# Second MLP layer and overlap-add as one convolution on TensorE, and patch rows that are loaded earlier, in the last phase of a two-layer image kernel

## The reference, cut to what matters

```python
def _mlp(x, W1, b1, W2, b2):
    h = jax.nn.relu(x @ W1.T + b1)
    return h @ W2.T + b2
B, C, H, W = x.shape                       # 16, 32, 64, 64
...
t = pat.reshape(B, C * 9, H * W).transpose(0, 2, 1)
t = t + _dmha(_ln2(t), Wr, Wqkv, Wp, bp)   # attention: the phase before
t = t + _mlp(_ln2(t), W1, b1, W2, b2)      # 288 -> 72 -> 288
y = t.transpose(0, 2, 1).reshape(B, C, 9, H, W)
out = jnp.zeros((B, C, H + 2, W + 2), x.dtype)
idx = 0
for i in range(3):
    for j in range(3):
        out = out.at[:, :, i:i + H, j:j + W].add(y[:, :, idx])
        idx += 1
return out[:, :, 1:H + 1, 1:W + 1]
...
x = x + _L1_conv_ref(_gn(x), ...)
```

## Time and profile before

| | us |
|---|---|
| median of 3 runs | 12895.44 |
| lowest, highest of them | 12892.05, 12903.24 |
| profiled execution | 12904.24 |
| its span, first to last instruction | 12902.4 |
| fold phase: first product of `hide` to the last `out` | 12141.63 to 12896.39 |
| one sample in it | 46.97 |

### The profile page before, as it was taken

How to read it: one execution, slowest core, us unless ns; L and a number is a source line. 1 busy time by engine, 2 the same in 40 slices (tenths; PEclk the granted TensorE clock), 3 DMA queues, 4 the chain that set the end, 5 groups by cost and what they waited for, 6 DMA issues and landing times. The chain is left out here.

```text
span 12902.4 us, 255523 instructions
## 1 busy us (share of the span) xinstructions
PE 12303.8 (95%) x73276; PEld 4675.7 (36%) x73276; DVE 9188.1 (71%) x17067; ACT 7592.3 (59%) x15286; POOL 3414.9 (26%) x3268
## 2 busy tenths in 40 slices
PE   6999999999993799999999999999999999999899
PEld 2333333333331233333333333333333333333233
DVE  6777777777776677777777777777777777777311
ACT  4666666666663366666666666666666666666411
POOL 4777777767772000000000000000000000000143
PEclk9999999999996799999999999999999999999999
DMA  3111111101104332232232232232232233232255
GB/s 78 22 20 18 22 19 19 22 17 21 22 15 131 74 72 67 68 73 67 67 74 67 66 75 67 66 75 67 65 75 68 65 74 69 65 73 68 68 122 111
DMA packets 853483, 772.61 MB, mean 60 GB/s; under 512 B 587092, under 2 KB 621492, under 8 KB 840884
## 3 DMA queue, kind: packets, MB, share of 16 engines
q1 hardware_dynamic: 850612, 747.43, 25.5%
q10 hardware_dynamic: 1536, 8.39, 0.3%
HBM read 510.63 MB, written 244.96 MB: 59 GB/s over the span
## 5 line engine op out<-in xcount | busy, mean ns | idle before, releaser
L1547 DVE TENSOR_REDUCE a_big<-a_mp 128x1 f32<-128x512 f32 x8192 | 5219.2, 684 | 1826.1 <-PE a_mp L1381 1807.4
L1467 ACT ACTIVATE a_ex<-a_sc 128x512 f32<-128x512 f32 x8192 | 4426.3, 601 | 1935.5 <-PE a_sc L1369 1930.6
L1381 PE MATMUL a_mp<-a_ks,a_qs 108*128 108x512 bf16 x8192 | 3131.1, 383 | 39.7 <-DMA a_ks<-qk_parts 24.9
L1369 PE MATMUL a_sc<-a_qs,a_ks 111*128 111x512 bf16 x8192 | 3124.5, 383 | 6.8 <-ACT a_ex L1467 4.5
L893 DVE TENSOR_TENSOR r_prod<-r_pg,r_win 128x512 f32<-128x512 f32 x2816 | 1846.1, 683 | 783.2 <-PE r_pg L618 438.6
L546 POOL TENSOR_TENSOR r_prod<-r_temp,r_win 128x512 f32<-128x512 f32 x1792 | 2095.8, 1189 | 1158.9 <-ACT r_temp L845 954.5
L1283 POOL TENSOR_TENSOR a_pieces<-a_left,a_pieces 128x512 bf16<-128x512 f32 x256 | 295.5, 1154 | 7323.9 <-ACT a_pieces L1453 7323.9
L1395 PE MATMUL a_po<-a_ex,a_va 128*32 128x512 f32 x16384 | 2182.0, 605 | 1.6 <-ACT a_oc L1473 0.9
L1369 PEld LDWEIGHTS a_sc<-a_qs,a_ks 111*128 111x128 bf16 x8192 | 794.9, 97 | 2477.4 <-ACT a_ex L1467 1767.8
L1381 PEld LDWEIGHTS a_mp<-a_ks,a_qs 108*128 108x128 bf16 x8192 | 803.1, 98 | 914.1 <-DVE a_big L1547 238.3
L845 ACT COPY r_temp<-r_pg 128x512 f32<-128x512 f32 x1792 | 975.3, 590 | 77.2 <-PE r_pg L618 38.6
(11 more groups left out here) (185 smaller groups left out, 11641.8 us busy)
## 6 DMA issues: line engine op xcount, KB each, us to landing
a_qs<-qk_parts SPq DMA_DIRECT2D x768, 144.0 KB
a_ks<-qk_parts SPq DMA_DIRECT2D x768, 144.0 KB
qk_parts<-a_pieces SPq DMA_DIRECT2D x128, 768.0 KB, 5.2
f_t<-mixed SPq DMA_DIRECT2D x48, 1536.0 KB, 16.6
a_tw<-second SPq DMA_DIRECT2D x512, 128.0 KB, 3.0
mixed<-a_t SPq DMA_DIRECT2D x256, 256.0 KB, 2.1
r_win<-first SPq DMA_DIRECT2D x128, 280.5 KB, 4.9
a_zw<-layered SPq DMA_DIRECT2D x192, 144.0 KB, 12.0
```

Source lines behind the costliest of these rows:

```text
L1369: pe.matmul(sc[k % BANKS][:, :], ks[0:KROWS + NPART, p.h, head, 128 * kb:128 * kb + 128], qs[0:KROWS + NPART, p.h, head, CHUNK * qb:CHUNK ...
L1381: pe.matmul(mp[k % BANKS][:, :], qs[0:KROWS, p.h, head, 128 * q:128 * q + 128], ks[0:KROWS, p.h, head, CHUNK * half:CHUNK * half + CHUNK], ...
L1467: nc.scalar.activation(ex[:, k % RING, :], sc[k % BANKS][:, :], ACT.Exp, scale=scale).then_inc(exped.sem, 1)
L1547: nc.vector.tensor_reduce(big[:, x % 2, k // 2:k // 2 + 1], mp[k % BANKS][:, :], AX_X, ALU.max).then_inc(maxed.sem, 1)
```

## The change

The second layer and the folding become one convolution: `fold` now has, ahead of the twelve products with `sel`, 36 products that read `hidden` shifted by patch row i and patch column j with the 96 by 32 part of W2 for (i, j), into the same `pf[q]`. `unhide`, the PSUM tiles `pw` and VectorE's sum into `u` go away. `three` takes the place of `u`: it holds all eight chunks with an empty column left and right, and is what `sel` reads. `hidden` becomes 66 by 66 and is held twice, for two samples. `ph` has four banks, where it had two.

The semaphore of the load is divided: `t_in` counts the three transfers of `t`, `x_in` the four of the image. SyncE's loop waits for the last sum of `three` of sample p, issues the loads of `t` for p + 2, then stores p, then loads the image for p + 2. GpSimd's last sum waits for the last product of the first layer, so that both readers of `t` are done by then. VectorE zeroes the wider tiles at the start.

```diff
-        def unhide(p, k):
-            pe.wait_ge(h_done.sem, h_done.at(p.n, min(k + 2, CHUNKS)))
-            pe.wait_ge(u_done.sem, u_done.at(p.n, k - 1))
-            for i in range(3):
-                first = (CROWS * k + 2 - i) * IMG
-                last = pe.matmul(pw[k % 2][0:ROWS3, :], w2[:, i, :], hidden[:, first:first + CHUNK],
-                                 start=i == 0, stop=i == 2)
-            last.then_inc(w_made.sem, 1)
-
         def fold(p, q):
-            pe.wait_ge(u_done.sem, u_done.at(p.n, LANES * (q + 1)))
+            pe.wait_ge(h_done.sem, h_done.at(p.n, min(LANES * (q + 1) + 1, CHUNKS)))
+            pe.wait_ge(summed.sem, summed.at(p.n, LANES * (q + 1)))
             pe.wait_ge(out_done.sem, out_done.at(p.n, q - 1))
+            for j in range(3):
+                for i in range(3):
+                    for l in range(LANES):
+                        row = CROWS * (LANES * q + l) + 2 - i
+                        pe.matmul(pf[q][C * l:C * l + C, :].rearrange("p (a b) -> p a b", b=IMG), w2[:, i, C * j:C * j + C],
+                                  hidden[:, p.h, row:row + CROWS, 2 - j:2 - j + IMG], start=i == j == 0, stop=False,
+                                  tile_position=(0, C * l))
             for j in range(3):
                 for l in range(LANES):
                     last = pe.matmul(pf[q][C * l:C * l + C, :].rearrange("p (a b) -> p a b", b=IMG), sel[:, j, :],
-                                     u[:, LANES * q + l, :, 2 - j:2 - j + IMG], start=j == 0, stop=j == 2,
+                                     three[:, LANES * q + l, :, 2 - j:2 - j + IMG], start=False, stop=j == 2,
                                      tile_position=(0, C * l))
...
         def sample(p):
-            for k in range(CHUNKS + 2):
-                if k < CHUNKS:
-                    hide(p, k)
-                if k == 2 and not (isinstance(p.n, int) and p.n == 0):
+            for k in range(CHUNKS):
+                hide(p, k)
+                if k == 1 and not (isinstance(p.n, int) and p.n == 0):
                     fold(p.to(-1), 1)
-                if k == CHUNKS - 1:
+                if k == CHUNKS - 2:
                     fold(p, 0)
-                if k >= 2:
-                    unhide(p, k - 2)
...
             with sp.Fori(0, samples // 2 - 1) as i:
                 for h in range(2):
-                    store(Pass(2 * i + h, h, i))
+                    p = Pass(2 * i + h, h, i)
+                    sp.wait_ge(summed.sem, summed.at(p.n, CHUNKS))
                     load(Pass(2 * i + 2 + h, h, i + 1))
+                    store(p)
+                    load_image(Pass(2 * i + 2 + h, h, i + 1))
...
-                pool.wait_ge(u_done.sem, u_done.at(p.n, k - 3))
-                nc.gpsimd.tensor_tensor(three[:, k % 4, :], two[:, :], t[:, p.h, 2, rows[2]],
+                pool.wait_ge(folded.sem, folded.at(p.n, k // LANES - 1))
+                if k == CHUNKS - 1:
+
+                    pool.wait_ge(h_made.sem, h_made.at(p.n, CHUNKS))
+                nc.gpsimd.tensor_tensor(three[:, k, :, 1:IMG + 1], two[:, :].rearrange("p (a b) -> p a b", b=IMG),
+                                        t[:, p.h, 2, rows[2]].rearrange("p (a b) -> p a b", b=IMG),
                                         ALU.add).then_inc(summed.sem, 1)
...
-        link(nc.vector.memset(hidden[:, :], 0.0))
-        link(nc.vector.memset(hidden[64:ROWS3, IMG:IMG + PIX], 1.0))
-        link(nc.vector.memset(u[:, :, :, :], 0.0))
+        link(nc.vector.memset(hidden[:, :, :, :], 0.0))
+        for h in range(2):
+            link(nc.vector.memset(hidden[64:ROWS3, h, 1:IMG + 1, 1:IMG + 1], 1.0))
...
             for k, of in enumerate((rstd, bias)):
                 nc.vector.tensor_copy(coef[0:HID, p.h, k:k + 1], of[0:HID, bass.ds(p.n, 1)]).then_inc(coef_ready.sem, 1)
-            for k in range(CHUNKS):
-                dve.wait_ge(w_made.sem, w_made.at(p.n, k + 1))
-                dve.wait_ge(summed.sem, summed.at(p.n, k + 1))
-                if k % LANES == 0:
-
-                    dve.wait_ge(folded.sem, folded.at(p.n, k // LANES - 1))
-                nc.vector.tensor_tensor(u[:, k, :, 1:IMG + 1], pw[k % 2][0:ROWS3, :].rearrange("p (a b) -> p a b", b=IMG),
-                                        three[:, k % 4, :].rearrange("p (a b) -> p a b", b=IMG),
-                                        ALU.add).then_inc(u_done.sem, 1)
-                if k == 0 and not (isinstance(p.n, int) and p.n == 0):
-                    finish(p.to(-1), 1)
-                if k == CHUNKS - 2:
-                    finish(p, 0)
+            dve.wait_ge(x_in[p.h].sem, x_in[p.h].at(p.m, 64))
+            if not (isinstance(p.n, int) and p.n == 0):
+                finish(p.to(-1), 1)
+            finish(p, 0)
```

More of the change, by code:

```diff
@@ L1599, in fold_phase @@
     t = sb("t", [ROWS3, 2, 3, PAD * IMG])
-    hidden = sb("hidden", [ROWS3, PAD * IMG])
-    three = sb("three", [ROWS3, 4, CHUNK])
+    hidden = sb("hidden", [ROWS3, 2, PAD, PAD])
     two = sb("two", [ROWS3, CHUNK])
-    u = sb("u", [ROWS3, CHUNKS, CROWS, PAD])
+    three = sb("three", [ROWS3, CHUNKS, CROWS, PAD])
     x1 = sb("x1", [128, 2, 2, CHUNK])
@@ L1623, in fold_phase @@
     coef = sb("coef", [ROWS3, 2, 2])
-    ph = [ctx.enter_context(nc.psum_tensor(f"f_ph{i}", [128, CHUNK], F32)) for i in range(2)]
-    pw = [ctx.enter_context(nc.psum_tensor(f"f_pw{i}", [128, CHUNK], F32)) for i in range(2)]
+    ph = [ctx.enter_context(nc.psum_tensor(f"f_ph{i}", [128, CHUNK], F32)) for i in range(4)]
     pf = [ctx.enter_context(nc.psum_tensor(f"f_pf{i}", [128, CHUNK], F32)) for i in range(2)]
@@ L1637, in fold_phase @@
     coef_ready = Signal(sem("coef_ready"), 2)
-    loaded = [Signal(sem(f"loaded{h}"), 16 * 7) for h in range(2)]
+    t_in = [Signal(sem(f"t_in{h}"), 48) for h in range(2)]
+    x_in = [Signal(sem(f"x_in{h}"), 64) for h in range(2)]
     h_made = Signal(sem("h_made"), CHUNKS)
     h_done = Signal(sem("h_done"), CHUNKS, 1)
-    w_made = Signal(sem("w_made"), CHUNKS)
     paired = Signal(sem("paired"), CHUNKS, 1)
     summed = Signal(sem("summed"), CHUNKS, 1)
-    u_done = Signal(sem("u_done"), CHUNKS, 1)
     folded = Signal(sem("folded"), 2, 1)
@@ L1669, in load, with load_image @@
                 sp.dma_start(t[:, p.h, i, IMG:IMG + PIX].rearrange("p (u x) -> p u x", u=4),
-                             src).then_inc(loaded[p.h].sem, 16)
+                             src).then_inc(t_in[p.h].sem, 16)
+        def load_image(p):
             image = total[bass.ds(C * p.n, C), :].rearrange("c (q l x) -> c l q x", l=LANES, x=CHUNK)
             for l in range(LANES):
-                sp.dma_start(x1[C * l:C * l + C, p.h, :, :], image[:, l, :, :]).then_inc(loaded[p.h].sem, 16)
+                sp.dma_start(x1[C * l:C * l + C, p.h, :, :], image[:, l, :, :]).then_inc(x_in[p.h].sem, 16)
         def store(p):
@@ L1679, in store @@
                 sp.dma_start(image[:, l, :, :], out[C * l:C * l + C, p.h, :, :]).then_inc(stored[p.h].sem, 16)
-        sp.wait_ge(edged, 6)
-        load(Pass(0, 0, 0))
-        load(Pass(1, 1, 0))
+        sp.wait_ge(edged, 7)
+        for h in range(2):
+            load(Pass(h, h, 0))
+            load_image(Pass(h, h, 0))
         if samples > 2:
@@ L1706, in hide @@
             if k == 0:
-                pe.wait_ge(loaded[p.h].sem, loaded[p.h].at(p.m, 16 * 7))
-            pe.wait_ge(h_done.sem, h_done.at(p.n, k - 1))
+                pe.wait_ge(t_in[p.h].sem, t_in[p.h].at(p.m, 48))
+            pe.wait_ge(h_done.sem, h_done.at(p.n, k - 3))
             for i in range(3):
                 first = (CROWS * k + 1) * IMG
-                last = pe.matmul(ph[k % 2][0:HID, :], w1[:, i, :], t[:, p.h, i, first:first + CHUNK],
+                last = pe.matmul(ph[k % 4][0:HID, :], w1[:, i, :], t[:, p.h, i, first:first + CHUNK],
                                  start=i == 0, stop=i == 2)
             last.then_inc(h_made.sem, 1)
-        def unhide(p, k):
-            pe.wait_ge(h_done.sem, h_done.at(p.n, min(k + 2, CHUNKS)))
-            pe.wait_ge(u_done.sem, u_done.at(p.n, k - 1))
-            for i in range(3):
-                first = (CROWS * k + 2 - i) * IMG
-                last = pe.matmul(pw[k % 2][0:ROWS3, :], w2[:, i, :], hidden[:, first:first + CHUNK],
-                                 start=i == 0, stop=i == 2)
-            last.then_inc(w_made.sem, 1)
         def fold(p, q):
-            pe.wait_ge(u_done.sem, u_done.at(p.n, LANES * (q + 1)))
+            pe.wait_ge(h_done.sem, h_done.at(p.n, min(LANES * (q + 1) + 1, CHUNKS)))
+            pe.wait_ge(summed.sem, summed.at(p.n, LANES * (q + 1)))
             pe.wait_ge(out_done.sem, out_done.at(p.n, q - 1))
+            for j in range(3):
[5 more added lines that the diff above has]
+                                  tile_position=(0, C * l))
             for j in range(3):
@@ L1765, in sample @@
                 act.wait_ge(h_made.sem, h_made.at(p.n, k + 1))
-                first = (CROWS * k + 1) * IMG
```

(10 more changed lines are left out.)

3 lines of the change are left out of this document (1 added, 2 removed).

## The result

| | before | after |
|---|---|---|
| median, us (6 runs each) | 12897.93 | 12812.45 |
| lowest, highest | 12892.05, 12905.04 | 12807.30, 12815.64 |
| span of the profiled execution | 12902.4 | 12810.0 |

The ratio after / before is 0.9933, with a 95% interval of 0.992 to 0.9946: 85 us or 0.7% faster. Forecast were 12812 and faster, in a range of 12800 to 12830.

The account below looks back on a forecast made before the run. TensorE alone was taken to set the period. 12904.24 - 82.4 (passes) - 2.3 (start) + 0.8 (last wait) = 12820.3 us profiled; 83.9 off the median gave 12812, range 12800 to 12830.

Parts of the forecast that it names:

- The pace of a group in lanes: TensorE's folding: four lane passes of 512 columns take 0.429 us together, also with 24 groups in a row.
- the far end: Upper price for four lane passes, 0.533 us, from the attention's lane passes, eight at a time between other products.
- rivals 1 and 2: Folding's lane groups: 1, pace lost in long runs, 12892 us, chance 0.08; 2, lanes not side by side, 13141, chance 0.03.
- The period: TensorE's time per sample in the fold phase: 41.82 us in place of 46.97, 82.4 us less over 16 samples.
- The load: Load of `t`, issued earlier by SyncE: earns nothing itself; left late, TensorE would wait some 3 us per sample.
- rival 3: Load of `t` late after all, some 3 us per sample, 48 us lost: 12860 us; chance 0.05.
- GpSimd and ScalarE: Writes with a step: GpSimd's sum between 1.26 us and twice that, ScalarE's at most twice 773 ns; both hidden.
- Both new waits of GpSimd: GpSimd's sums wait for the previous sample's foldings, its last sum for the last `hide`; hidden from TensorE in the loop.
- Start and end: First product 2.3 us earlier, no longer waiting for the image; preparation grows 3.9 us; nothing changes behind the last folding.
- the last wait: Last folding of the last sample waits 1.7 us for GpSimd in place of 0.87, costing 0.8 us.
- Rival 4: TensorE's loop body, grown to 240 calls, is fetched anew: a few us at most over seven turns, inside the range.

## Why the prediction was right

**The pace of a group in lanes.** This was the step on which the sum rested, 0.429 from a run of six groups, with 0.533 as the far end. It is 0.429 in runs of 24 groups and of 42, and with it rivals 1 and 2 fall. The 0.533 of the earlier trace rows is 0.1 more per group in pairs of groups, 0.2 per pair, which is of the size of a turn into the lanes and out (0.29); I haven't tested that it is one. The trace disagrees with the 60 cycles per matmul that the Trainium skill gives (TensorEngine Tiling (Array Packing), Instruction Overhead) if they are added over lanes: four lane passes take 0.429 us together.

**The period.** 41.82 by the sum, 41.78 measured; the turns cost 0.29 and not 0.31. Over 16 samples 83.0 us by the periods, 82.4 in the prediction.

**The load.** Right in its place and its need: with the load late, TensorE waits, and alone the early load is worth nothing. What the prediction named as the price of a late load, some 3 us per sample, was mis-sized: it is 4.1 us, 2.6 for the wait and, on average, 1.5 for the slow passes behind nine of the 14 waits. This didn't touch the forecast, in which the wait doesn't occur, but rival 3's 12860 would have been 12868.

**GpSimd and ScalarE.** No row showed a write with a step on either; 1268 and 777 ns are within 1% of the plain form, at the low end of the range that I had given. Both new waits of GpSimd show: 2.0 us per sample for the second folding, and 18 us for the last `hide`, the one that was to place the load. In the loop, neither holds TensorE up.

**Start and end.** The first product was forecast 2.3 us earlier; against the first transfer of weights it is 27.59 in place of 30.02, 2.4 earlier. The memset of the ones with a step takes 3472 ns, as the plain one, so that the preparation ended at 12128.1, ahead of the load; it grew by 4.6 us, where 3.9 were forecast. What the sum had at nothing is the cold start. TensorE begins the phase at a granted clock of 0.50, and in the changed kernel the first eight passes are slow, up to 0.89 us each, where in the kernel before they are six. They cost 3.3 us over the pace of 0.429 in place of 2.3, so that of the 2.4 us by which the first product is earlier, 1.0 is lost again. Why they are two more no run shows. The last folding waits 1.53 us for 1.7 forecast, and the row names ScalarE where I had named GpSimd: both end close to each other, 12792.10 + 1.26 for the sum.

**The loop.** No wait of TensorE shows at a turn of the loop, whose body went from 144 to 240 calls; all periods are alike. Rival 4's few us are zero.

No step failed that the forecast stands on. In the phase the sum gave 83.9 us and the profiles give 83.8: 83.0 from the periods (82.4 forecast), 2.4 from the start (2.3), less 0.7 for the last wait (0.8), less 1.0 for the cold start, which the sum didn't have. That the errors cancel to 0.1 is luck, and so is it that the median came out within 1 us of the forecast: the median of the kernel before moved by 2.5 us from three runs to six.

## What to carry to other kernels

A product whose output is narrow is worth putting in column lanes with its neighbours, if the lanes take turns product by product; here four then cost what one costs, in runs of up to 42 groups. Count passes, not calls: the second layer cost less with 72 calls per sample than with 24, since four of them share a pass of the array. Before shortening the engine that bounds, look at the margin of every load that is asked for by the old period: here it was 1.7 us against a gain of 5.2, and without the move two thirds of the gain would have gone.

## What the runs showed of the hardware

Of 14 pauses of TensorE of 2.0 to 3.9 us, nine were followed by five to eight slow passes (0.855 us at the lower level of the clock in place of 0.429), mostly from the first pass on, and five by none; the slow passes cost 21.2 us beside 36.2 us for the pauses. With products on constants in the pause the clock stayed at 1.00, and the kernel with more work was 13 us faster in the phase. TensorE starts products of a free lane about four passes ahead of their turn, not more. Going into the lanes and out of them costs 0.29 us.
